# One non-local block and one attention block over four images: phi folded into theta, side work through one PSUM bank, one order of steps for all tiles

## The chip, the cores and the metric

The kernel runs on one core of one Trainium2 chip. The metric is the device time of one execution in microseconds (us), the median of several runs. The core has a matrix engine (TensorE; PE for its matmuls, PEld for its weight loads), VectorE (DVE), ScalarE (ACT), GpSimd (POOL) and SyncE (SP, which here only issues DMAs). Each engine works through its own list of instructions in order and waits on semaphores that the others raise.

## The reference

`x` is four images of 128 channels by 1024 pixels, float32. Two layers follow each other.

```python
# layer 0, per image, 64 inner channels, N = 1024
g_x     = conv1x1(x, g_w, g_b)^T          # N x 64
theta_x = conv1x1(x, theta_w, theta_b)^T  # N x 64
phi_x   = conv1x1(x, phi_w, phi_b)        # 64 x N
y   = (theta_x @ phi_x / N) @ g_x
z   = x + conv1x1(y^T, out_w, out_b)

# layer 1, per image, 128 channels
theta = conv1x1(z, theta_w, theta_b)
phi   = conv1x1(z, phi_w, phi_b)
scores = einsum('ncp,ncq->npq', theta, phi) / sqrt(128)
attn   = softmax(scores, axis=-1)
f      = einsum('npq,ncq->ncp', attn, z)
out    = z + conv1x1(f, conv1_w, conv1_b)
```

Layer 0 has no softmax, so it is an affine map of x once the 64 x 64 product phi_x g_x is known. Both kernels use that: Z = A x + d, with A and d made from that product for each image.

## The kernel before

**Layer 0 of an image.** `phi_g` (L208) multiplies the pixels with the joined phi and g weights; VectorE adds the bias into `pgT` (L660). `inner_product` (L219) forms the 64 x 64 product M; ScalarE copies it. `out_times_inner` (L230) and `fold` (L237 to L239) turn it into A (transposed) and d. `fold_x` forms A x; ScalarE writes `Z` (L535).

**Precision by splitting.** A float32 operand of a large matmul is split into a high part in the type fp32r and a low rest (`X_hi`, `X_lo`, and so on), and the product is made in three passes of fp32r (`three_passes`, L254). ScalarE or GpSimd writes the high part, VectorE or GpSimd the low part.

**Layer 1.** `theta` and `phi` make T and Phi from Z, each by three passes and each split again. The value matrix V (`values`, L262) is conv1_w applied to Z, so that the last convolution needs no work of its own. An image has eight tiles of 128 query pixels. For each tile t:

- PE `scores(t)`: six matmuls of 512 columns into a slot of `ring` (two banks to a slot);
- DVE `row_max` (L695) over 1024 columns, then ACT `exps` (L567), which writes `P` and the row sums, then DVE `norm` (L701, L703: reciprocal, then P times it);
- PE `turn` (L304): eight transposes of 128 x 128 into `turned`, in two halves of four;
- ACT `high_turned` (L576) and DVE `low_turned` (L710), one for each half, make `PT_hi` and `PT_lo`;
- PE `attend` (L334): after four tiles, a group, 24 matmuls of 512 columns in four pieces of six into `numer`; ScalarE copies `numer` to `attended`, GpSimd adds `Zres` (Z plus the bias) and SyncE stores.

**Order.** The lists of the engines are written out by hand. The side work for image b+1 (phi_g, M, R, A, A x, theta, phi) and V of image b stand between the tiles of image b. The middle images run in a hardware loop. PSUM is a `ring` of three slots of two banks (the third slot is split into `numer` and `small`) and `turned`. The side work takes ring slots 0 and 1 in turn with the scores, by the table `S_SLOT`. In a steady step the lists are:

- ACT: `high_turned(t-2, 0)`, `exps(t)`, `high_turned(t-2, 1)`;
- DVE: `row_max(t+1)`, `low_turned(t-1, 0)`, `norm(t)`, `low_turned(t-1, 1)`.

So a row maximum may be taken while the two engines are still at the transposes of an older tile, and the exponentials of a tile stand between the two high halves. PE stands up to two tiles of scores ahead (`scores(0)` to `scores(3)` of image 0 are issued before the first transpose). The last image's last group is finished by `attend_last` on 384 columns (L317) and a last tile in plain float32 (L495).

## Time and profile before

| | |
|---|---|
| median of 3 runs | 178.74 us (178.66 to 178.77) |
| span of the profiled execution | 176.7 us |
| PE busy | 170.2 us, 96% of the span |
| DVE busy | 131.4 us, 74% |
| ACT busy | 103.1 us, 58% |
| POOL busy | 35.8 us, 20% |
| chain that ended last | PE 83%, DVE 5%, ACT 5%, DMA 4% |

The profile is one execution. Its span runs from the first to the last instruction; the device time is about 2.0 us longer (178.74 less 176.7). Busy time of PE overstates its work, since a matmul's record also covers the pipeline behind it: what a matmul takes of the engine is read better from the distance between starts, which the chain of waits gives.

### The profile page before, as it was taken

The page shows a single profiled execution, that of the slowest core. Times are in us where ns is not written, and L with a number is a line of the kernel's source. Part 1 is how long each engine was busy: PE and PEld are TensorE (multiplying, and loading weights), DVE is VectorE, ACT ScalarE, POOL GpSimd, SP SyncE. Part 2 cuts the span into 40 slices and gives each one's busy share as a digit, 9 for nine tenths or more (in the row PEclk, how much of TensorE's full clock was granted, in tenths as well). Part 3 has the DMA queues.
Part 4 walks back from the last instruction along what each step waited for, and adds up shares of the span by engine and source line. Part 5 has one row for each costly group of instructions (what it writes and reads, how often), then busy time and mean ns, then how long its engine had stood idle before and what let it go on. Part 6 is the DMA issues. An engine that isn't in the chain of part 4 may idle for free.

```text
span 176.7 us, 2720 instructions
## 1 busy us (share of the span) xinstructions
PE 170.2 (96%) x974; PEld 138.9 (79%) x974; DVE 131.4 (74%) x189; ACT 103.1 (58%) x176; POOL 35.8 (20%) x32
## 2 busy tenths in 40 slices
PE   7899998999999999999999999999999999998994
PEld 7784585788889887888889787988888888876794
DVE  0315889886987776896988676796989689899811
ACT  3024477858683365958684274958686557656410
POOL 1105600003102200543202200443302202340000
PEclk9999999999999999999999999999999999999999
DMA  4600000003001000013001000010000100100011
GB/s 137 190 0 0 4 0 0 0 4 118 1 2 59 2 4 0 0 59 91 32 0 57 3 0 0 0 59 0 0 0 18 41 4 0 59 2 0 0 63 59
DMA packets 2537, 4.71 MB, mean 27 GB/s; under 512 B 288, under 2 KB 992, under 8 KB 2528
## 3 DMA queue, kind: packets, MB, share of 16 engines
q1 hardware_dynamic: 2096, 4.26, 7.1%
q10 hardware_dynamic: 432, 0.33, 0.8%
q8 instruction: 6, 0.10, 0.2%
q14 instruction: 3, 0.02, 0.1%
HBM read 2.49 MB, written 2.10 MB: 26 GB/s over the span
## 4 chain that ended last, share of the span: by engine, by line
PE 83%; DVE 5%; ACT 5%; DMA 4%; SPq 1%; issue 1%; ACTq 0%; DVEq 0%
PE ring L254 29%; PE ring L334 21%; PE turned L304 14%; PE ring L262 4%; DMA X<-x_dram 4%; ACT P L567 3%; PE ring L244 3%; PE ring L317 3%; PE ring L208 2%; DVE negmax L695 2%; DVE PT_lo L710 2%; ACT PT_hi L576 2%; PE ring L219 2%; PE turned L208 1%; PE ring L495 1%; PE ring L288 1%
## 5 line engine op out<-in xcount | busy, mean ns | idle before, releaser
L576 ACT ACTIVATE PT_hi<-turned 128x512 fp32r<-128x512 f32 x62 | 35.9, 595 | 26.5 <-PE turned L304 26.5
L695 DVE TENSOR_REDUCE negmax<-ring 128x1 f32<-128x1024 f32 x32 | 39.1, 1222 | 15.3 <-PE ring L254 15.1
L567 ACT ACTIVATE P<-ring,negmax 128x1024 f32<-128x1024 f32 x32 | 35.8, 1118 | 19.0 <-DVE negmax L695 19.0
L710 DVE TENSOR_TENSOR PT_lo<-turned,PT_hi 128x512 fp32r<-128x512 f32 x62 | 42.1, 684 | 5.2 <-ACT PT_hi L576 4.7
L304 PE MATMUL turned<-identity,P 128*128 128x128 f32 x256 | 36.1, 274 | 2.1 <-DVE P L703 1.6
L304 PEld LDWEIGHTS turned<-identity,P 128*128 128x128 f32 x256 | 30.4, 141 | 9.0 <-DVE P L703 1.6
L703 DVE TENSOR_SCALAR P<-P,rden 128x1024 f32<-128x1024 f32 x32 | 27.0, 845 | 1.1
L334 PE MATMUL ring<-PT_hi,V_hi 128*128 128x512 f32 x56 | 23.5, 420 | 0.1
L334 PE MATMUL ring<-PT_lo,V_hi 128*128 128x512 f32 x56 | 22.2, 396 | 0.0
L334 PE MATMUL ring<-PT_hi,V_lo 128*128 128x512 f32 x56 | 22.1, 395 | 0.0
L254 PE MATMUL ring<-Phi_hi,T_hi 128*128 128x512 f32 x62 | 21.3, 424 | 0.0
L254 PE MATMUL ring<-Phi_hi,T_lo 128*128 128x512 f32 x62 | 19.4, 394 | 0.0
L254 PE MATMUL ring<-Phi_lo,T_hi 128*128 128x512 f32 x62 | 19.3, 392 | 0.0
L835 POOL TENSOR_TENSOR result<-attended,Zres 128x512 f32<-128x512 f32 x6 | 8.6, 1432 | 37.4 <-ACT attended L583 37.4
L254 PEld LDWEIGHTS ring<-Phi_lo,T_hi 128*128 128x128 f32 x62 | 11.6, 188 | 2.7
L254 PEld LDWEIGHTS ring<-Phi_hi,T_lo 128*128 128x128 f32 x62 | 11.6, 188 | 2.7
L811 POOL TENSOR_TENSOR Z_lo<-Z,Z_hi 128x1024 fp32r<-128x1024 f32 x3 | 7.2, 2397 | 27.7 <-ACT Z_hi L541 27.7
L334 PEld LDWEIGHTS ring<-PT_hi,V_hi 128*128 128x128 f32 x56 | 10.5, 188 | 2.8 <-issue 0.6
L806 POOL TENSOR_TENSOR X_lo<-X,X_hi 128x1024 fp32r<-128x1024 f32 x3 | 7.1, 2367 | 26.9 <-ACT X_hi L527 26.9
L334 PEld LDWEIGHTS ring<-PT_hi,V_lo 128*128 128x128 f32 x56 | 10.5, 188 | 2.5
L254 PEld LDWEIGHTS ring<-Phi_hi,T_hi 128*128 128x128 f32 x62 | 10.1, 189 | 2.2 <-DVE T_lo L675 0.3
L334 PEld LDWEIGHTS ring<-PT_lo,V_hi 128*128 128x128 f32 x56 | 10.6, 189 | 1.6
(101 smaller groups left out, 200.3 us busy)
## 6 DMA issues: line engine op xcount, KB each, us to landing
out_dram<-result SPq DMA_DIRECT2D x7, 256.0 KB, 2.0
X<-x_dram SPq DMA_DIRECT2D x3, 512.0 KB, 3.3
X_first<-x_dram SPq DMA_DIRECT2D x2, 256.0 KB, 4.1
w<-weights_dram ACTq DMA_DIRECT2D x1, 194.0 KB, 5.8
out_dram<-result SPq DMA_DIRECT2D x1, 192.0 KB, 1.9
wi<-inner_dram SPq DMA_DIRECT2D x1, 64.2 KB, 5.9
pg_w<-pg_weights_dram ACTq DMA_DIRECT2D x1, 64.0 KB, 3.2
pg_b<-pg_bias_dram ACTq DMA_DIRECT2D x1, 64.0 KB, 5.5
```

Of the source, the lines that this page charges most:

```text
L254: mm = nc.tensor.matmul(ring[:, slot, columns(h)], left, right[:, columns(h)], start=(n == 0), stop=(n == 2))
L262: mm = nc.tensor.matmul(ring[:, slot, j * C:(j + 1) * C], Z[:, j * TILE:(j + 1) * TILE], w[:, W_C:W_C + C], start=True, stop=True)
L304: mm = nc.tensor.transpose(turned[:, j * TILE:(j + 1) * TILE], P[:, t % P_BUFFERS, j * TILE:(j + 1) * TILE], identity[:, :])
L334: mm = nc.tensor.matmul(numer[:, :], left[:, chunk], right[:, g, j, :], start=(j == 0 and n == 0), stop=(j == TILES - 1 and n == 2))
L567: nc.scalar.activation(P[:, t % P_BUFFERS, :], ring[:, slots[t], :], ACT.Exp, bias=negmax[:, t:t + 1], accum_out=den[:, t:t + 1]).then_inc ...
L576: nc.scalar.activation(PT_hi[:, g, half_chunks(h), k * TILE:(k + 1) * TILE], turned[:, columns(h)].rearrange("p (j r) -> p j r", j=CHUNKS_ ...
L695: nc.vector.tensor_reduce(negmax[:, t:t + 1], ring[:, slots[t], :], AX.X, ALU.max, negate=True).then_inc(max_ready, 1)
L703: nc.vector.tensor_scalar(P[:, t % P_BUFFERS, :], P[:, t % P_BUFFERS, :], rden[:, t:t + 1], None, ALU.mult).then_inc(probs_normed, 1)
L710: nc.vector.tensor_tensor(PT_lo[:, g, half_chunks(h), rows], turned[:, columns(h)].rearrange("p (j r) -> p j r", j=CHUNKS_PER_HALF), PT_hi ...
L806: nc.gpsimd.tensor_tensor(X_lo[:, :], X[:, :], X_hi[:, :].bitcast(F32), ALU.subtract).then_inc(x_lo, 1)
L811: nc.gpsimd.tensor_tensor(Z_lo[:, :], Z[:, :], Z_hi[:, :].bitcast(F32), ALU.subtract).then_inc(z_lo, 1)
L835: nc.gpsimd.tensor_tensor(result[:, g, :], attended[:, g, :], Zres[:, columns(g)], ALU.add).then_inc(result_ready, 1)
```

## The change

The kernel is written anew around the same arithmetic of A, Z, V and attention.

1. **Phi goes into theta.** The scores of a query p against all q are z_p^T (theta_w^T phi_w) z_q plus a term that depends on q alone plus terms constant in q. The kernel makes U = theta_w^T phi_w (scaled) once, at the start, with two transposes and a few small matmuls, and from then on `t = U^T Z + u` takes the place of T, and Z itself the place of Phi. The `phi` passes and `high_phi`/`low_phi` are gone. The term `rho` in p comes as an extra column of the V matmul (130 columns a chunk, one of them zero, instead of 128); a new VectorE instruction per tile combines it with the row maximum into `shift`, the bias of the exponential. (`shift` subtracts and adds `rho` again, and so carries the rounding of the maximum.)
2. **One bank for side work.** A bank `aux` of 512 columns takes all side work of the next image, in twelve jobs in a fixed order; each waits until the one before it is out of the bank (`aux_free`). The ring has two slots, for scores alone, used in turn. V of image b+1 is now made during image b, in three parts.
3. **One step for all tiles.** All 32 tiles run the same lists, unrolled. GpSimd now writes both parts of X and Z (`split_x`, `split_z`); `Zres` is gone, and the last bias is added when ScalarE copies `numer`.
4. **The first image** makes A x and t by three passes too (before: plain float32), and needs V for its first tile.

The core of the diff (the new three loops with what they call; "..." where lines are left out):

```diff
+JOBS = ("pg0", "pg1", "MT", "R", "A", "Z0", "Z1", "t0", "V0", "V1", "V2", "t1")
-        ring = ctx.enter_context(nc.psum_tensor("ring", [C, 3, PIX], F32))
-        S_SLOT = [1, 0, 1, 1, 0, 0, 0, 1]
+        ring = ctx.enter_context(nc.psum_tensor("ring", [C, 2, PIX], F32))
+        aux = ctx.enter_context(nc.psum_tensor("aux", [C, BANK], F32))
...
         def _(pe):
+            def job_pg(b, half):
+                pe.wait_ge(aux_free, aux_before(b, f"pg{half}"))
...
+            def scores(n):
...
+                if n >= 2:
+                    pe.wait_ge(probs_ready, n - 1)
+                for half in range(HALVES):
+                    if n == 0:
+                        pe.wait_ge(first_z_lo, half + 1)
+                    mm = scores_half(n, half)
+                mm.then_inc(scores_ready, 1)
+            def turn(n, half):
+                if half == 0:
+                    pe.wait_ge(probs_normed, n + 1)
+                if n >= 1:
+                    pe.wait_ge(turned_lo, (n - 1) * HALVES + half + 1)
...
+            job_t(0, 1)
+            pe.wait_ge(first_z_ready, 2)
+            scores(1)
+            for part in (1, 2):
+                pe.wait_ge(first_v_lo, part)
+                value_chunks(0, numer, part).then_inc(first_v, 1)
...
+            for n in range(ALL - 1):
+                b, t = divmod(n, TILES)
+                turn(n, 0)
+                if b + 1 < IMAGES:
+                    job_one(b + 1, t)
+                if n + 2 < ALL:
+                    scores(n + 2)
+                turn(n, 1)
+                if b + 1 < IMAGES:
+                    job_two(b + 1, t)
+                if n >= GT:
+                    attend(n // GT - 1, n % GT)
+            attend(ALL_GROUPS - 2, PIECES - 1)
...
         def _(act):
+            def exps(n):
+                t = n % TILES
+                if n >= P_BUFFERS:
+                    act.wait_ge(turned_ready, (n - P_BUFFERS + 1) * HALVES)
+                act.wait_ge(shift_ready, n + 1)
+                nc.scalar.activation(P[:, n % P_BUFFERS, :], ring[:, n % 2, :], ACT.Exp, bias=shift[:, t:t + 1],
+                                     accum_out=den[:, t:t + 1]).then_inc(probs_ready, 1)
...
+            high_t(0, 1)
+            exps(0)
+            exps(1)
+            first_v_high(1)
+            first_v_high(2)
...
+            for n in range(ALL - 1):
+                b, t = divmod(n, TILES)
+                high_turned(n, 0)
+                if b + 1 < IMAGES:
+                    job_one(b + 1, t)
+                high_turned(n, 1)
+                if b + 1 < IMAGES:
+                    job_two(b + 1, t)
+                if n + 2 < ALL:
+                    exps(n + 2)
+                if n >= GT and n % GT == GT - 1:
+                    copy_numer(n // GT - 1)
...
         def _(dve):
+            def row_max(n):
+                b, t = divmod(n, TILES)
+                dve.wait_ge(scores_ready, n + 1)
+                nc.vector.tensor_reduce(negmax[:, t:t + 1], ring[:, n % 2, :], AX.X, ALU.max,
+                                        negate=True).then_inc(max_ready, 1)
...
+                dve.wait_ge(max_ready, n + 1)
+                nc.vector.tensor_scalar(shift[:, t:t + 1], negmax[:, t:t + 1], rho[:, b % 2, t:t + 1],
+                                        rho[:, b % 2, t:t + 1], ALU.subtract, ALU.add).then_inc(shift_ready, 1)
...
+            first_z_low(0)
+            first_t_low(0)
+            first_z_low(1)
+            first_v_low(0)
+            first_t_low(1)
+            row_max(0)
+            low_t(0, 1)
+            row_max(1)
+            norm(0)
+            first_v_low(1)
+            first_v_low(2)
...
+            for n in range(ALL - 1):
+                b, t = divmod(n, TILES)
+                low_turned(n, 0)
+                if b + 1 < IMAGES:
+                    job_one(b + 1, t)
+                norm(n + 1)
+                if n + 2 < ALL:
+                    row_max(n + 2)
+                low_turned(n, 1)
+                if b + 1 < IMAGES:
+                    job_two(b + 1, t)
```

`job_one` and `job_two` are small functions that pick the side work of a step by its tile t, on each engine:

| t | PE one / two | ACT one / two | DVE one / two |
|---|---|---|---|
| 0 | pg0 / pg1 | none | pgT copy half 0 / half 1 |
| 1 | M / R | M copy / R copy | none |
| 2 | A / Z half 0 | high A / Z half 0 | d and low A / none |
| 3 | Z half 1 / t half 0 | Z half 1 / high t half 0 | none / low t half 0 |
| 4 | V part 0 / part 1 | high V 0 / high V 1 | low V 0 / low V 1 |
| 5 | V part 2 / t half 1 | high V 2 / high t half 1 | low V 2 / low t half 1 |

`attend`, `norm`, `high_turned` and `low_turned` do what they did before; `copy_numer` has become the instruction that also adds the bias.

## Rows read from the trace of the kernel before

**Rows 1.** The page: busy time per engine, and TensorE's granted clock in 40 slices.

```profile
PE 170.2 (96%) x974; PEld 138.9 (79%) x974; DVE 131.4 (74%) x189; ACT 103.1 (58%) x176; POOL 35.8 (20%) x32
...
PEclk9999999999999999999999999999999999999999
```

**Rows 2.** Chain that ended last, image 1 as current: start us, us, engine tile line.

```profile
53.27 1.78 PE ring L208 x16
55.05 0.87 PE turned L304 x8
55.92 1.38 PE ring L254 x6
57.30 1.41 PE ring L334 x6
...
65.15 1.08 PE ring L219 x16
66.23 1.59 PE ring L254 x6
...
70.09 0.41 PE ring L230 x2
...
72.97 1.79 PE ring L262 x16
...
75.90 1.58 PE ring L254 x6
...
93.54 1.78 PE ring L208 x16
```

**Rows 3.** Timeline, tile work of image 0: start us, us, engine, line, operation.

```profile
25.51 0.60 ACT L576 ACTIVATE PT_hi<-turned 128x512 fp32r<-128x512 f32 x1 [0.72 <-PE turned L304]
...
26.14 0.69 DVE L710 TENSOR_TENSOR PT_lo<-turned,PT_hi 128x512 fp32r<-128x512 f32 x1 [0.60 <-ACT PT_hi L576]
26.75 0.15 DVE L701 RECIPROCAL rden<-den 128x1 f32<-128x1 f32 x1
26.94 0.75 DVE L703 TENSOR_SCALAR P<-P,rden 128x1024 f32<-128x1024 f32 x1
...
28.33 1.21 DVE L695 TENSOR_REDUCE negmax<-ring 128x1 f32<-128x1024 f32 x1
...
29.58 1.12 ACT L567 ACTIVATE P<-ring,negmax 128x1024 f32<-128x1024 f32 x1 [0.53 <-DVE negmax L695]
...
30.69 0.59 ACT L576 ACTIVATE PT_hi<-turned 128x512 fp32r<-128x512 f32 x1
```

**Rows 4.** Chain that ended last, one turn through ACT and DVE in image 3.

```profile
158.92 1.21 ACT P L567 x2
...
162.56 1.21 ACT P L567 x2
```

**Rows 5.** The page: the group of the normalisation; count, busy us, mean ns of one.

```profile
L703 DVE TENSOR_SCALAR P<-P,rden 128x1024 f32<-128x1024 f32 x32 | 27.0, 845 | 1.1
```

**Rows 6.** Timeline, image 3: a GpSimd pass and the normalisation that runs beside it.

```profile
154.13 2.40 POOL L853 TENSOR_TENSOR V_last<-V_hi,V_lo 128x1024 f32<-128x1024 f32 x1 [0.75 <-DVE V_lo L689]
...
155.89 1.19 DVE L703 TENSOR_SCALAR P<-P,rden 128x1024 f32<-128x1024 f32 x1
```

**Rows 7.** Timeline, start: d of image 0, the first halves of T, the first transposes.

```profile
12.77 0.26 ACT L520 ACTIVATE d<-ring,w 128x1 f32<-128x1 f32 x1 [1.51 <-PE ring L239]
...
16.51 0.69 ACT L545 ACTIVATE T_hi<-ring,w 128x512 fp32r<-128x512 f32 x1 [2.18 <-PE ring L244]
...
17.23 0.75 DVE L675 SCALAR_TENSOR_TENSOR T_lo<-ring,w,T_hi 128x512 fp32r<-128x512 f32 x1 [0.62 <-ACT T_hi L545]
...
24.88 1.03 PE L304 MATMUL turned<-identity,P 128*128 128x128 f32 x8
```

**Rows 8.** Chain that ended last, its end: the last group and the last tile.

```profile
167.11 1.33 PE ring L317 x6
...
174.29 0.02 issue
```

More of the change, by code:

```diff
@@ L189, in _ @@
[L189 to L196 removed]
+            for half in range(HALVES):
+                sp.dma_start(X[:, 0, columns(half)], x[0, :, columns(half)]).then_inc(first_loaded[half], 16)
@@ new lines, in store @@
+            def store(b, g):
+                sp.wait_ge(result_ready, b * GROUPS + g + 1)
+                sp.dma_start(out[b, :, columns(g)], result[:, g, :]).then_inc(stored[g], 16)
+            load(2)
+            for b in range(IMAGES):
+                if b + 3 < IMAGES:
+                    load(b + 3)
+                store(b, 0)
+                if b < IMAGES - 1:
+                    store(b, 1)
+            b, g = IMAGES - 1, GROUPS - 1
+            for part, cols in enumerate((slice(0, LAST_COLS), slice(LAST_COLS, BANK))):
+                sp.wait_ge(last_ready, part + 1)
+                sp.dma_start(out[b, :, BANK + cols.start:BANK + cols.stop],
@@ new lines, in job_t, with value_chunks @@
+            def job_t(b, half):
+                pe.wait_ge(aux_free, aux_before(b, f"t{half}"))
+                if b:
+                    pe.wait_ge(z_lo, (b - 1) * HALVES + half + 1)
+                queries(b, aux[:, :], columns(half)).then_inc(aux_ready, 1)
+            def value_chunks(b, bank, part):
+                first, last = V_PARTS[part]
+                for j in range(first, last):
+                    at = (j - first) * V_COLS
+                    mm = nc.tensor.matmul(bank[:, at:at + V_COLS], Z[:, b % Z_BUFFERS, j * TILE:(j + 1) * TILE],
+                                          VW[:, :], start=True, stop=True)
+                return mm
@@ L306, in turn @@
                 mm.then_inc(turned_ready, 1)
-            def turn_tile(b, t, first=False):
-                for h in range(HALVES):
-                    turn(b, t, h, first)
-            def attend_last(j):
-                rows = slice(0, LAST_COLS)
-                chunk = slice(j * C, (j + 1) * C)
-                for n, (left, right) in enumerate(((V_hi, PT_hi), (V_hi, PT_lo), (V_lo, PT_hi))):
-                    mm = nc.tensor.matmul(last_rows, left[:, chunk], right[:, GROUPS - 1, j, rows],
-                                          start=(j == 0 and n == 0), stop=(j == TILES - 1 and n == 2))
-                return mm
```

1017 lines of the change are left out of this document (466 added, 551 removed).

## Prediction, made blind

> **What bounds the kernel now.** I read the page first. PE is busy for 96% of the span, and its granted clock stands at the full level in every slice [rows 1]. Busy time alone says little, so the chain of waits comes next: in the middle images it is one unbroken row of PE pieces, each starting where the last ended, from 53.27 to 93.54, which is one image, 40.27 us [rows 2]. Nothing but PE's work sets the time there. The distances give each piece's price: eight transposes 0.87, six score matmuls 1.38, six attention matmuls 1.41; phi_g 1.78, M 1.08, R 0.41, V 1.79, and A with d from 74.76 (where V ends) to 75.90, so 1.14 [rows 2]. Score matmuls right behind M or A take 1.6, some 0.2 more. In the first and the last image the chain leaves PE: it turns through ACT and DVE, and one such turn is 162.56 - 158.92 = 3.64 us a tile [rows 4], about what PE needs for a tile (0.87 + 1.38 + 1.41 = 3.66). So before the change the hand-made order holds two limits at almost the same height, and whatever lengthens the turn through ACT and DVE by a microsecond makes that turn the limit.
>
> **PE's own sum.** Gone are three times six matmuls of 512 columns for phi, 3 x 1.4 = 4.2 us, and image 0's float32 pass for it. Added: 2 columns in 130 for V, under 0.03 an image, and at the start two transposes and the small matmuls of U, near 1.3 us, which stand where R and A would wait anyway. Side work for one image is then 1.78 + 1.08 + 0.41 + 1.14 + 1.4 (A x) + 1.4 (t) + 1.8 (V) = 9.0 us. With eight tiles, 8 x 3.66 = 29.3, an image asks 38.3 us of PE, some 39 with the 0.2 behind each change of type, against 40.3 now. If PE stayed the bound, the kernel would win 1 to 2 us an image.
>
> **The turn through ACT and DVE.** Now the lists of the changed kernel. Step n on DVE is low half of turn n, norm(n+1), row_max(n+2), shift, second low half. On ACT it is high half of turn n, second high half, exps(n+2). Both are in order, which closes a ring: high(n,0) lets low(n,0) go; behind it in DVE's list stand norm(n+1) and row_max(n+2); shift(n+2) releases exps(n+2); and behind that in ACT's list stands high(n+1,0). No buffer opens this ring, since it lies in the order of the lists. The timeline gives each link as a distance between starts [rows 3]: high to low 26.14 - 25.51 = 0.63; low to reciprocal 0.61; reciprocal to multiplication 0.19; the multiplication 0.75, less the 0.08 by which a successor on the same engine may start early (0.69 against 0.61), 0.67; row maximum to exponential 29.58 - 28.33 = 1.25; exponential to the next high half 30.69 - 29.58 = 1.11. Together 4.46. The shift is new. Its nearest row is the reciprocal, as small (128x1), 0.15 and 0.19 to its successor; I take 0.19. It can't be below nothing, since the exponential waits for it; above I allow twice the reciprocal's distance, 0.38. Over 30 steps these ends are 6 us less and 6 us more. The ring is thus 4.65 us. The old turn of 3.64 held neither the norm nor the shift (0.86 + 0.19), and that is the difference: 3.64 + 1.05 = 4.69.
>
> The multiplication averages 0.845 over the kernel [rows 5] against 0.75 alone, and took 1.19 at 155.89, while GpSimd ran a pass from 154.13 to 156.53 [rows 6]. GpSimd now has more to do (both parts of X and Z), and the change puts the multiplication into the ring. I take 0.03 to 0.1 a step for it, ring 4.7. The Trainium skill, page "GPSIMD Engine Reference", says of the memory interfaces that they are shared with VectorE, with contention for its instructions in a two-port mode or with two SBUF inputs; by that rule every multiplication that meets one of GpSimd's passes would be slow, and none of the low halves (which read one operand from PSUM). The trace agrees on the multiplication. By the rule applied in full to GpSimd's longer day, 0.15 a step would be nearer than 0.05, 3 us in all.
>
> A step without side work is therefore 4.7 us and no longer 3.66: PE is idle for one microsecond in each.
>
> **What side work adds to the ring.** On DVE the first job of a step stands between low(n,0) and norm(n+1), so inside it. A pgT copy of 512 columns is as large as a low half, 0.61; low A with d, by the line through 0.15 (1 column) and 0.69 (512), 0.3; V parts 0 and 2, with the rho instruction, 0.6 and 0.45. That is 2.0 us an image. The copy of `numer` on ACT stands between exps and the next high half every fourth step: 0.5. The moves to GpSimd (high X, high Z) free ACT, which is not what the ring waits for. POOL's list has a store wait and 2 to 3 us passes, but it runs three jobs ahead of their use.
>
> **What the one bank adds.** PE may lag behind the ring by at most 4.65 - 2.3 - 0.7 = 1.7 us (norm(n+1) is done 2.3 after high(n,0), and a transpose half is readable 0.63 to 0.7 after it starts). Waits for `aux_free` eat that. I worked the lists through for one middle image, times from its first transpose, high(0,0) at 2.9:
>
> - t=0: pg0 is in the bank by 1.6, but DVE comes to its copy behind low(0,0) and frees it at 4.85. PE has stood at pg1 since 3.16 and everything behind it, attention and the next transposes, moves: they start at 7.15. The ring asks for 8.15 (2.9 + 4.65 + 0.6).
> - t=1: pg1 is freed behind row_max and the low half, at 8.3; M runs to 9.4, scores(3) behind it to 10.97, so row_max(3) starts at 11.07 in place of 10.3. R follows, PE turns the next tile at 13.4, high(2,0) at 14.1.
> - t=2 to 5: 19.8, 25.3 (with a `numer` copy), 30.5, 35.7; A's low part and V's low parts lie in the ring, and V2 waits 0.9 for V1. Then 40.4 and, with the second `numer` copy, 45.5.
>
> So a middle image takes 45.5 - 2.9 = 42.6 us, of which 8 x 4.7 + 2.0 + 1.0 = 40.6 are the ring and 2.0 the bank. Before: 40.3.
>
> **Start.** d of image 0 was ready at 12.77 [rows 7]; the chain to it is the same but for U, and the high and low parts of A are there at about 13.2. From there: first half of A x 0.95 (0.7 and the pipeline), Z high 0.69, Z low 0.75 [both rows 7], 15.6; t for tile 0, its two parts behind ACT's copy of Z, 16.9; second half of Z low 17.6; scores(0) readable 18.7. DVE then has in its list V's first part 19.2, t low 20.4, row_max 21.6, t low half 1 22.4, row_max(1) 23.7, norm 24.6. PE issues scores(1) by 21.8 and then stands at V part 2, which needs part 1's low half, which ACT begins only behind exps(1), at 24.9: 25.4, 26.0, V part 2 26.5, the first transposes 26.5 and high(0,0) at 27.2. Before, the first transposes were at 24.88 [rows 7], with two more tiles of scores behind them. The stop of PE here is hidden by nothing.
>
> **End.** From high(30,0): low, norm, second low, 2.9; then attend_last, the last turn and the last tile as now, 174.29 - 167.11 = 7.18 [rows 8]; then 176.7 - 174.29 = 2.4. Sum 12.4.
>
> **Sum.** Start 27.2; image 0 (side work but no attention in its first half, `numer` once) 40.8; images 1 and 2 2 x 42.6 = 85.2; tiles 24 to 29 6 x 4.7 + 0.5 = 28.7; end 12.4. Span 194.3, against 176.7 now. The device time is 2.0 above the span (178.74 - 176.7), so 196.3 us. The largest single loss is the last image: it has no side work left to hide in, and its eight steps go from 3.66 to 4.7.
>
> **Rivals.**
> PE stays the bound (the other side). Place: the steps of all images; it decides if high(n+1,0) does not in fact wait for exps(n+2), or if PE's queue of work fills the ring's idle time. Then start 26.5, 31 steps of tile work and three images of side work 135, type changes 3, end 7.2 + 2.4: span about 174, 176 us. The unbroken PE chain now speaks for it; the order of ACT's list against it. 3%.
> The ring without the bank: PE's waits are absorbed by its slack, steps at 4.65. Start 26.5, 30 x 4.65 = 139.5, `numer` 3, DVE's jobs 6, end 12.4: 187.4, 189.5 us. For it: 1.7 us of slack. Against: two jobs in one step need the bank freed twice by engines that come to it late. 17%.
> The bank costs more: each of the 18 steps with jobs is 0.4 longer than worked out, since the wait for the bank delays the scores and so the row maximum, as at t=1 above, or GpSimd's passes delay Z low and every multiplication. 194.3 + 7, 203 us. 15%.
> The clock falls: with PE idle a microsecond a step and 4 us at the start, the granted clock goes to 1.2 GHz, a tile costs PE 7.3 and the span grows by 31 x (7.3 - 4.7) = 80. In the trace the clock stays full through the idle of the first image [rows 1]. 2%. Beside this stands the Trainium skill, page "TensorE: Matmul & The Clock Gate", section "HAM oscillation", by which idle between bursts of matmuls throttles the engine again; gaps here are short and many.
>
> **How the numbers follow.** Forecast as summed 63%, within 191 and 200. The range takes in the light rival at 189 and most of the heavy one: 189 to 203. A difference under 0.2% can't be told from none. Faster only by the first rival, 3%; within 0.2% 1%; slower 96%.
>
> **What would show it.** Right: in tiles 24 to 29 high halves of new tiles start 4.6 to 4.8 us apart; the chain there runs ACT, DVE, DVE, DVE, ACT and hardly touches PE; the row maximum there waits for DVE's own list and not for PE; PE waits at `turned` for the norm; in steps with t=0 PE waits for pgT's copy; first high half at 27. Wrong: PE still unbroken in the middle images; a middle image under 41 or over 45; a clock below full.

## The result, and the profile after

The changed kernel takes 207.91 us (median of 4 runs, 205.63 to 208.72) against 178.75 for the kernel before: a ratio of 1.159 (95% interval 1.153 to 1.165; ratios here leave out executions more than 1.5% above the fastest of their kernel, in this case the one of 208.72). The forecast was 196.3 with a range of 189 to 203. The direction is right; the size is 4.9 us beyond the upper end. The profiled execution spans 206.2 us, where the sum said 194.3: 11.9 us are to be explained.

The page of the changed kernel (busy line; granted clock in 40 slices; the chain's shares by engine; two groups with count, busy us, mean ns | idle before and what ended most of it):

```profile
PE 174.5 (85%) x969; PEld 139.6 (68%) x969; DVE 139.4 (68%) x253; ACT 99.4 (48%) x183; POOL 35.4 (17%) x34
...
PEclk9999959999699987999999969999999999999999
...
DVE 37%; PE 36%; ACT 18%; issue 4%; DMA 2%; DVEq 0%; ACTq 0%; SPq 0%
...
L510 ACT ACTIVATE P<-ring,shift 128x1024 f32<-128x1024 f32 x32 | 35.7, 1116 | 48.6 <-DVE shift L669 48.5
...
L677 DVE TENSOR_SCALAR P<-P,rden 128x1024 f32<-128x1024 f32 x32 | 27.5, 861 | 1.1
```

PE has gone from 96% of the span [rows 1] to 85%. ScalarE stands for 48.5 us at the new shift instruction. And the clock, full in every slice before [rows 1], is not full in five.

The chain of waits in a stretch without side work (start us, us, what), where before stood an unbroken row of PE pieces [rows 2]:

```profile
61.81 1.21 ACT P L510 x2
63.02 0.50 ACT PT_hi L518
...
63.54 0.69 DVE PT_lo L684
64.23 0.08 DVE rden L675
...
64.33 0.75 DVE P L677
65.09 1.14 DVE negmax L661
...
66.33 0.28 DVE shift L669
...
66.70 1.21 ACT P L510 x2
67.90 0.50 ACT PT_hi L518
```

From one high half to the next (63.02 to 67.90) are 4.88 us, and no PE piece is among them: this is the ring that was forecast. The timeline of the same place shows the link that was not sized right (start us, us, engine, line, operation):

```profile
69.89 1.22 DVE L661 TENSOR_REDUCE negmax<-ring 128x1 f32<-128x1024 f32 x1
71.21 0.27 DVE L669 TENSOR_SCALAR shift<-negmax,rho 128x1 f32<-128x1 f32 x1
...
71.58 1.12 ACT L510 ACTIVATE P<-ring,shift 128x1024 f32<-128x1024 f32 x1 [2.70 <-DVE shift L669]
```

From the row maximum to the exponential are 1.69 us, against 1.25 before [rows 3]: the shift costs 0.44 in the ring, 0.27 for itself and the rest because it starts only when the maximum is out of the pipeline, 1.32 behind the maximum's start.

Where the 11.9 us lie, by the start of each image's first high half:

| stretch | forecast | measured | difference |
|---|---|---|---|
| start to high(0,0) | 27.2 | 27.7 | 0.5 |
| image 0 | 40.8 | 45.5 | 4.7 |
| images 1 and 2 | 42.6 each | 44.2, 44.3 | 3.3 |
| tiles 24 to 29 | 28.7 | 32.1 | 3.4 |
| end | 12.4 | 12.4 | 0 |

Two places stand out. In image 3 one multiplication takes 2.91 us beside a pass of GpSimd (timeline):

```profile
163.16 2.91 DVE L677 TENSOR_SCALAR P<-P,rden 128x1024 f32<-128x1024 f32 x1
...
163.17 2.35 POOL L829 TENSOR_TENSOR V_last<-V_hi,V_lo 128x1024 f32<-128x1024 f32 x1
```

It ends 0.55 behind GpSimd's pass (166.07 against 165.52), which is nearly its whole own length of 0.75. Before, the one that took 1.19 ended 0.55 behind the pass as well (157.08 against 156.53) [rows 6]. So it isn't slowed: it stands until the pass is over. That step takes 7.06 in place of 4.88. A pass that only casts does the same on a smaller scale:

```profile
91.80 0.61 POOL L805 CAST Z_hi<-Z 128x512 fp32r<-128x512 f32 x1 [0.53 <-ACT Z L485]
91.91 1.05 DVE L677 TENSOR_SCALAR P<-P,rden 128x1024 f32<-128x1024 f32 x1
```

Again the multiplication ends 0.55 behind the pass (92.96 against 92.41).

And PE stands at the second half of phi_g at the head of images 1 and 2, and then runs at half clock (timeline of PE; behind it the table of windows: us, busy by engine, granted clock, DMA share and GB/s):

```profile
72.80 0.60 PE L316 MATMUL turned<-identity,P 128*128 128x128 f32 x4
75.22 1.40 PE L226 MATMUL aux<-pg_w,X 128*128 128x128 f32 x8 [1.82 <-DVE pgT L625]
76.28 0.78 PE L336 MATMUL numer<-PT_hi,V_hi 128*128 128x512 f32 x1
76.85 0.63 PE L336 MATMUL numer<-PT_lo,V_hi 128*128 128x512 f32 x1
77.28 0.63 PE L336 MATMUL numer<-PT_hi,V_lo 128*128 128x512 f32 x1
```

```profile
26.00:36.00 10.00, 8.87 (x55) 7.93 (x55) 6.19 (x12) 3.34 (x7) 0.00 (x0) 0.72 0.03 5
52.00:56.00 4.00, 4.00 (x18) 3.46 (x16) 3.53 (x7) 0.97 (x3) 0.00 (x0) 0.57 0.00 0
61.00:71.00 10.00, 9.29 (x53) 7.35 (x52) 7.93 (x14) 4.71 (x9) 0.00 (x0) 1.00 0.00 0
73.00:83.00 10.00, 8.18 (x50) 6.54 (x48) 6.93 (x12) 3.42 (x8) 4.95 (x3) 0.83 0.07 26
```

The attention matmuls at 77 start 0.43 apart and not 0.23, so the clock is at the lower of its two levels, 1.2 and not 2.4 GHz. There are four such stretches inside the kernel, one of 6.8 us at the start and three of 3.4, at 52.1, 76.0 and 120.4: 17.1 us at half. The four executions don't share one clock: the one of 208.05 us, which is profiled here, had a mean clock of 0.957, the one of 205.63 had 0.975. The ordinary steps at 61 to 71, in which PE lacks more than a microsecond each (4.88 less 3.66) in pieces under 0.9 us, keep the full clock.

### The profile page after: what moved, and what is told of

It is laid out like the page before. It is cut to its first block, busy times and chain, and to the rows that moved or that the text cites. A ratio compares the mean times of both kernels' runs of the same rounds, so it can differ in the third digit from the quotient of the medians.

```text
span 206.2 us, 2628 instructions
## 1 busy us (share of the span) xinstructions
PE 174.5 (85%) x969; PEld 139.6 (68%) x969; DVE 139.4 (68%) x253; ACT 99.4 (48%) x183; POOL 35.4 (17%) x34
## 4 chain that ended last, share of the span: by engine, by line
DVE 37%; PE 36%; ACT 18%; issue 4%; DMA 2%; DVEq 0%; ACTq 0%; SPq 0%
DVE negmax L661 13%; ACT P L510 9%; PE numer L336 9%; DVE P L677 8%; DVE PT_lo L684 8%; ACT PT_hi L518 5%; PE turned L316 5%; PE ring L220 3%; DVE shift L669 3%; PE ring L221 3%; PE ring L222 3%; DMA X<-x_dram 2%; PE aux L343 2%; PE aux L226 2%; PE aux L232 2%
## 5 line engine op out<-in xcount | busy, mean ns | idle before, releaser
L684 DVE TENSOR_TENSOR PT_lo<-turned,PT_hi 128x512 fp32r<-128x512 f32 x62 | 42.6, 687 | 35.5 <-ACT PT_hi L518 35.5
L510 ACT ACTIVATE P<-ring,shift 128x1024 f32<-128x1024 f32 x32 | 35.7, 1116 | 48.6 <-DVE shift L669 48.5
L316 PE MATMUL turned<-identity,P 128*128 128x128 f32 x256 | 40.8, 284 | 9.7 <-DVE P L677 7.8
L220 PE MATMUL ring<-Z_hi,t_hi 128*128 128x512 f32 x64 | 28.4, 444 | 0.7 <-DVE t_lo L721 0.7
L336 PE MATMUL numer<-PT_hi,V_hi 128*128 128x512 f32 x56 | 25.0, 447 | 1.3 <-issue 0.7
L222 PE MATMUL ring<-Z_lo,t_hi 128*128 128x512 f32 x64 | 25.9, 404 | 0.0
L221 PE MATMUL ring<-Z_hi,t_lo 128*128 128x512 f32 x64 | 25.8, 403 | 0.0
L336 PE MATMUL numer<-PT_lo,V_hi 128*128 128x512 f32 x56 | 23.0, 411 | 0.0
L336 PE MATMUL numer<-PT_hi,V_lo 128*128 128x512 f32 x56 | 23.0, 411 | 0.0
L220 PEld LDWEIGHTS ring<-Z_hi,t_hi 128*128 128x128 f32 x64 | 12.4, 193 | 3.1 <-issue 1.1
L222 PEld LDWEIGHTS ring<-Z_lo,t_hi 128*128 128x128 f32 x64 | 12.4, 194 | 2.9
L221 PEld LDWEIGHTS ring<-Z_hi,t_lo 128*128 128x128 f32 x64 | 12.5, 196 | 1.6
```

Of the source, the lines that this page charges most:

```text
L220: nc.tensor.matmul(to, left_hi, right_hi[:, cols], start=first, stop=False)
L221: nc.tensor.matmul(to, left_lo, right_hi[:, cols], start=False, stop=False)
L222: return nc.tensor.matmul(to, left_hi, right_lo[:, cols], start=False, stop=last)
L316: mm = nc.tensor.transpose(turned[:, j * TILE:(j + 1) * TILE], P[:, n % P_BUFFERS, j * TILE:(j + 1) * TILE], identity[:, :])
L336: mm = nc.tensor.matmul(numer[:, :], left[:, b % 2, chunk], right[:, g, j, :], start=(j == 0 and n == 0), stop=(j == TILES - 1 and n == 2))
L510: nc.scalar.activation(P[:, n % P_BUFFERS, :], ring[:, n % 2, :], ACT.Exp, bias=shift[:, t:t + 1], accum_out=den[:, t:t + 1]).then_inc(pro ...
```

## The experiments

All ratios are to the kernel before. A "pure" step is one without side work and without a `numer` copy. Edits are to the changed kernel unless said otherwise.

**1. No side work.** All tiles use image 0's t, Z and V.

```diff
-                if b + 1 < IMAGES:
+                if False:
                     job_one(b + 1, t)
```

> The changed kernel without the side work for images 1 to 3 (no pg, M, R, A, Z, t, V for them; all 32 tiles use image 0's t, Z and V), so only the tile steps are left. Ring theory (high half, low half, norm, row maximum, shift, exponential, next high half, each behind the other by the order of two lists): a step stays at the 4.88 us of tiles 25 to 29 of the changed kernel, although PE needs only 3.66 for it; from high(0,0) to high(30,0) 30 x 4.88 + 6 x 0.57 for the numer copies = 149.8, with 2 more for the V_last pass, span 27.7 + 152 + 12.4 = 192, 194 us. PE theory: steps of 3.66, span 155. The difference to the changed kernel, about 14 us, is then all that side work, bank and lowered clock together cost. If the clock matters on its own, it falls here too, since PE idles more, and steps in the low stretches take 7 instead of 4.9.

193.93 us, 1.083 (1.078 to 1.087); pure steps 4.81, images 39.6. With nothing but the ring, the kernel is still 15 us slower than before, which alone rules out "PE stays the bound". Side work, its bank and what they do to the clock are the other 14. The clock itself is no fuller here (mean 0.955, five stretches of 3.4 us). Two of them, at 35.8 and 46.0, follow PE waits of 2.06 and 2.11 in steps that have no attention yet, and there they cost little: the two steps at 35.8 take 4.82 and 4.88, the one at 46.0 takes 5.29, where 4.81 is usual.

**2. Open the ring at ScalarE.** The exponentials go ahead of the second high half, one step later, as the kernel before had them.

```diff
                 high_turned(n, 0)
+                if n >= 1:
+                    exps(n + 1)
...
-                if n + 2 < ALL:
-                    exps(n + 2)
```

> The changed kernel with the exponential moved on ACT from behind both high halves of step n to behind the first high half of step n+1, where the kernel before has it. Ring theory: the ring opens; what is left is exponential, norm, row maximum, shift, exponential, 1.2 + 0.86 + 1.69 = 3.8 us. Steps 24 to 29 go from 32.1 us to 25 (with the V_last stop), images 0 to 2 by 2 to 3 each, down to what PE and the bank allow (41 to 42 an image): 190 to 194 us. Bank theory: under 3 us in all, since images 1 and 2 wait for the bank. Clock theory: PE idles less, so fewer low stretches.

189.36 us, 1.057 (1.052 to 1.062). Pure steps fall from 4.88 to 3.80, images to 39.0, 41.0 and 41.0. 18.5 us come back by moving one line in one engine's list, with every instruction kept: most of the loss is this order. In the chain, between the transposes of two tiles of image 3 (3.81 us), PE stands alone again:

```profile
159.60 0.44 PE turned L316 x4
160.04 0.23 PE ring L220
...
161.43 0.57 PE turned L316 x4
162.00 1.40 PE numer L336 x6
163.41 0.44 PE turned L316 x4
```

**3. No shift.** The exponential takes the row maximum itself as its bias.

```diff
-                act.wait_ge(shift_ready, n + 1)
-                nc.scalar.activation(P[...], ring[...], ACT.Exp, bias=shift[:, t:t + 1],
+                act.wait_ge(max_ready, n + 1)
+                nc.scalar.activation(P[...], ring[...], ACT.Exp, bias=negmax[:, t:t + 1],
...
-                nc.vector.tensor_scalar(shift[:, t:t + 1], negmax[:, t:t + 1], rho[...],
-                                        rho[...], ALU.subtract, ALU.add).then_inc(shift_ready, 1)
```

> The changed kernel without the shift instruction; the exponential takes the negated maximum as its bias. Ring theory: shift's link (row maximum to exponential is 1.69 us with it, 1.25 without) goes from every step: 4.88 to 4.44, tiles 25 to 29 by 2.2 us, and most of the other steps, 8 to 12 us in all: 196 to 200 us. If images 1 and 2 are bound by PE and the bank, only the 14 steps without side work gain, 6 us: 202.

197.73 us (193.2 to 198.74; the executions differ in where the clock falls, so no ratio is given). The pure step is 4.50, against 4.88: the ring without the shift was forecast at 4.46, and the shift is worth 0.38 a step. The timeline, one round from low half to low half:

```profile
61.30 0.69 DVE L676 TENSOR_TENSOR PT_lo<-turned,PT_hi 128x512 fp32r<-128x512 f32 x1 [0.56 <-ACT PT_hi L518]
61.91 0.15 DVE L667 RECIPROCAL rden<-den 128x1 f32<-128x1 f32 x1
62.09 0.75 DVE L669 TENSOR_SCALAR P<-P,rden 128x1024 f32<-128x1024 f32 x1
62.76 1.22 DVE L661 TENSOR_REDUCE negmax<-ring 128x1 f32<-128x1024 f32 x1
63.90 0.68 DVE L676 TENSOR_TENSOR PT_lo<-turned,PT_hi 128x512 fp32r<-128x512 f32 x1
65.80 0.69 DVE L676 TENSOR_TENSOR PT_lo<-turned,PT_hi 128x512 fp32r<-128x512 f32 x1 [1.22 <-ACT PT_hi L518]
```

**4. The ring in the kernel before.** Its own arithmetic, slots and side work, but both vector engines' lists in the changed order.

```diff
                 for t in range(TILES - 1):
-                    row_max(b, t + 1, slots)
                     if t >= 1:
                         low_turned(b, t - 1, 0)
                     norm(b, t)
+                    row_max(b, t + 1, slots)
...
                     high_turned(b, t - 2, 0, has_prev)
+                    high_turned(b, t - 2, 1)
                     exps(b, t, has_prev, slots)
```

> The kernel before with nothing but the order of two lists changed to that of the changed kernel: on ACT the exponential behind both high halves, on DVE the norm ahead of the row maximum. Phi, slots and side work as before. Ring theory: the ring high, low, norm, row maximum, exponential (no shift here) takes 4.44 to 4.50 us; the last image's tiles go from 3.66 to 4.5, 6 us for eight; in images 0 to 2 PE needs 40 and the ring 8 x 4.5 = 36 plus about 4 for DVE's own side work inside it, so 0.5 to 1.5 more each: 185 to 189 us, and PE's unbroken chain is broken in the last image. If the loss came from the single bank or the first image, the order alone costs nothing: 179.

222.14 us, 1.244 (1.242 to 1.246). The pure step in the last image is 4.51, as in experiment 3, so the ring belongs to the order and not to the new arithmetic. But the whole was missed by over 30 us: images of 47.5, 51.2 and 49.7. With side work in the ring's own two slots, the late exponentials also hold those slots, and single steps take up to 8.7: PE waits up to 3.73 us for an exponential there. The clock also falls six times (mean 0.953); how much of the 30 us it makes isn't separated. With this order, the separate bank does better than the shared slots.

**5. Row maximum ahead of the norm.**

```diff
-                norm(n + 1)
                 if n + 2 < ALL:
                     row_max(n + 2)
+                norm(n + 1)
```

> The changed kernel with the row maximum and shift ahead of the norm on DVE. Ring theory: the ring to the exponential loses the norm (0.86) and falls to 4.02, but the transposes of the next tile now come behind row maximum and norm: 0.62 + 0.61 + 1.32 + 0.19 + 0.19 + 0.79 + 0.66 = 4.4 us a step becomes the ring. 0.48 less in the steps without side work, nearly as much in the others: 195 to 200 us. Against: if PE or the bank bound images 1 and 2, only 14 x 0.48 = 7 us at the most from image 3 and tiles 6 and 7.

207.8 us, 1.153 (1.144 to 1.162): nothing gained. Pure steps fall only to 4.60, and steps with side work grow (6.23 and 6.49 for t=0 and 1 of image 1). The chain of waits says why:

```profile
66.31 0.66 PE turned L316 x4
66.97 0.23 PE ring L220
...
68.12 0.25 PE ring L222
...
68.39 1.24 DVE negmax L661
...
69.72 0.27 DVE shift L669
70.00 0.08 DVE rden L675
...
70.10 0.76 DVE P L677
...
70.91 0.66 PE turned L316 x4
```

The norm now stands behind a row maximum that waits for PE's scores, and PE's next scores stand behind the transposes that wait for the norm. ScalarE is out of the ring, PE has come in, and that ring is 4.60.

**6. V_last late.** GpSimd makes it behind the last norm.

```diff
-                else:
-                    pool.wait_ge(aux_free, aux_after(i, "V2"))
-                    nc.gpsimd.tensor_tensor(V_last[:, :], ...).then_inc(v_joined, 1)
                 if i >= 1:
                     finish((i - 1) * GROUPS + 1)
+                if i + 1 == IMAGES:
+                    pool.wait_ge(probs_normed, ALL)
+                    nc.gpsimd.tensor_tensor(V_last[:, :], ...).then_inc(v_joined, 1)
```

> The changed kernel with GpSimd's V_last pass moved behind the last norm. In the changed kernel the multiplication that started at 163.16 beside this pass took 2.91 us and ended 0.55 behind it. If VectorE's multiplication can't run while GpSimd holds the memory interface, step 24 goes from 7.06 to 4.9 and the kernel gains 2.2: 205.7 us. If the 2.9 us had another cause, no change.

207.73 us, 1.163 (1.161 to 1.165). Step 24 falls from 7.06 to 4.90, so the stop of 2.2 us is shown. The time doesn't follow: the end takes 13.7 and not 12.4, and a new stretch at half clock lies there, at 191.6. That stretch need not come from the move. It follows a PE wait of 1.46 us, and behind the same wait one lies in experiment 8 too, where V_last stands in its old place and the end takes 13.8; in the changed kernel's trace the wait is there and the stretch is not.

**7. Idle matmuls before each turn.** PE is kept busy with 6 small matmuls ahead of each wait for the norm, and 60 at the start. They write into `turned`, so the wait for the last low half now stands ahead of them.

```diff
                 if half == 0:
+                    if n >= 1:
+                        fill(6)
                     pe.wait_ge(probs_normed, n + 1)
```

> The changed kernel with idle matmuls of 128 columns on PE (results overwritten): six ahead of each wait for the norm, sixty ahead of the wait for V part 2 at the start. Clock theory: the granted clock falls four times in the changed kernel (17.1 us at half), and its four runs give 129 us for 1.0 of mean clock, so 5.6 us for the 0.043 missing; with PE filled the clock stays full and the time is 202 to 203, unless the 0.35 us of filling per step delays the side work. Ring theory alone: no change beyond 1 us, since PE waits for the ring at either clock. If the drops come from the waits for the bank and not from those for the norm, they stay.

207.16 us, 1.156 (1.153 to 1.160); mean clock 0.974 in place of 0.957. Image 0 gets 1.2 shorter, image 1 stays at 44.3: t=0 falls to 5.70, but the filling delays later steps by 0.5 and less. Inconclusive on the clock's price, so experiment 13 puts the filling elsewhere.

**8. First copy of pgT ahead of the low half.**

```diff
+                if b + 1 < IMAGES and t == 0:
+                    job_one(b + 1, t)
                 low_turned(n, 0)
-                if b + 1 < IMAGES:
+                if b + 1 < IMAGES and t > 0:
                     job_one(b + 1, t)
```

> The changed kernel with DVE's copy of pg half 0 ahead of the low half of the same step. Bank theory: the copy leaves the ring (0.61) and PE no longer stands at pg half 1 (from 73.2 to 75.2 in image 1), M comes earlier and with it scores and row maximum of t=1: step t=0 from 6.6 to 5.0, t=1 from 5.5 to 5.2, 2 us an image, 6 in all, and the low stretches of the clock at 76 and 120 go: 201 to 202 us. If the bank costs nothing beyond the copy in the ring: 2 us in all, 206.

212.04 us, 1.185 (1.182 to 1.189): slower, the opposite of what was expected. t=0 falls from 6.58 to 5.72, and t=1 rises from 5.51 to 7.18. PE's wait has moved to the next job, and the half clock with it (timeline of PE, where M takes 1.73 and not 1.15):

```profile
80.51 1.73 PE L232 MATMUL aux<-pgT 128*64 128x64 f32 x16 [2.05 <-DVE pgT L625]
```

Of the 4.4 us by which this profiled execution is longer, images 1 and 2 make 1.5. The other 2.9 are start and end (high(0,0) at 29.2, end 13.8), where its trace has stretches at half clock, at 12.6 and 196.9, that the changed kernel's has not.

**9. Attention ahead of the second job.**

```diff
+                if n >= GT:
+                    attend(n // GT - 1, n % GT)
                 if b + 1 < IMAGES:
                     job_two(b + 1, t)
-                if n >= GT:
-                    attend(n // GT - 1, n % GT)
```

> The changed kernel with PE's attention piece ahead of the second job of each step in place of behind it. Bank theory: PE's wait for the bank (2.0 us at pg half 1, up to 1 at V part 2 and t half 1) is covered by the 1.4 us of attention, the next transposes are no longer late: t=0 from 6.6 to 5.9, t=2, 4 and 5 by 0.1 to 0.3; 1 to 1.5 us for images 1 and 2, nothing for image 0's first half: 205. Ring theory alone: under 1 us, since the ring sets the step and PE has slack.

216.37 us, 1.208 (1.201 to 1.215). Missed again, and instructive: t=0 falls to 5.74, but t=1 is 7.80, t=2 5.63 and t=3 6.24. The attention piece is what PE has to do while the second job gets out of the bank; ahead of it, two jobs stand with too little between them, and PE waits 2.05 us at the same M as above. So "attention last" is the right order for the one bank.

**10. Ring open and no shift** (edits 2 and 3 together).

> The changed kernel with the exponential back between the high halves and without shift. Ring theory: what is left of the ring is 3.80 - 0.38 = 3.42 us, below PE's 3.66, so steps without side work go to 3.66 and PE's chain closes there; steps with side work, 5.1 to 6.1 with the exponential alone moved, lose up to 0.3 each: 2 + 3 to 5 us below the 189.4 of that kernel: 183 to 186. If ring and bank were additive in full, 0.38 x 30 = 11: 178.

185.21 us, 1.024 (1.019 to 1.030). Pure steps 3.66, which is PE's own price for a tile: the ring is gone. In the profiled execution (186.53 us) the start is long, high(0,0) at 29.0 (29.9 in experiment 2), with two stretches of 6.8 us at half clock. One execution kept the full clock throughout and took 182.35.

**11 and 12. A shorter start.** V part 2 of image 0 moves into step 1 on all three engines, so that PE no longer waits ahead of the first transposes until part 1 is out of its bank; this on top of edits 2 and 3 and together with edit 9; then the same with 16 and 24 idle matmuls in the start.

```diff
+            first_values(1)
...
                 if b + 1 < IMAGES:
                     job_two(b + 1, t)
+                if n == 1:
+                    first_values(2)
```

> The changed kernel with the exponential back between the high halves, without shift, with attention ahead of the second job, and with V parts 1 and 2 of image 0 taken out of the way of the first transposes (part 2 goes into step 1). Start: high(0,0) from 27.7 to 24.5 or 25; images 0.5 to 1 us less each than without the last two edits: 178 to 181, about the kernel before. Rival: the V parts come back as waits in steps 0 and 1, and the gain of the start is given back there.

> As mid_vlate, with idle matmuls in the two idle stretches of PE at the start (sixteen before t of tile 0, twenty-four before the first transposes). Clock theory: the low stretches behind the start (6.8 us at 24.8 in the changed kernel) go, 1.5 to 2 us less than without, and the runs scatter less. If PE had slack there, no change.

184.72 us, 1.034 (1.032 to 1.036), and 185.12, 1.037 (1.033 to 1.040). high(0,0) comes at 24.3, but each middle image takes 41.8 in place of 40.2: edit 9 loses 3.2 us of the 4.8 that the start of the profiled executions gained. At full clock it loses more than the start gives, since the four executions of experiment 11 were all at full clock and took 184.4 to 185.1, against the one of 182.35 above. In neither trace is there a stretch at half clock, so the idle matmuls had nothing to mend there.

**13. Filling exactly where PE stands.** 60 idle matmuls in the start, 30 ahead of the second pg job, into the free ring slot.

```diff
                 if t == 0:
+                    n = (b - 1) * TILES
+                    pe.wait_ge(probs_ready, n + 2)
+                    for _ in range(30):
+                        nc.tensor.matmul(ring[:, (n + 1) % 2, 0:C], idle[:, :], idle[:, :], start=True, stop=True)
                     job_pg(b, 1)
```

> The changed kernel with idle 128-column matmuls on PE in two places where it stands long: 60 of them behind the wait for V part 1 at the start, 30 (into the free ring slot) ahead of the second pg job of each image, where PE waits for VectorE's copy of pgT. No wait and no order is changed. Theory A (the lowered clock costs some 0.9 us for each of the stretches at 52, 76 and 120 us and 1 to 1.8 at the start): the granted clock stays full, step t=0 goes from 6.6 to 5.7, image 0 from 45.5 to 43.5, and the time from 207.9 to 203 to 204.5. Theory B (the ring would wait anyway, the clock only falls where PE has time): the clock stays full and nothing moves by more than 1 us, 207 to 208.5. If the clock still falls somewhere, only the stretches that are gone tell.

205.22 us, 1.144 (1.140 to 1.147). PE of this kernel at the head of image 1 (timeline):

```profile
72.14 1.84 PE L421 MATMUL ring<-idle 128*128 128x128 bf16 x30
74.13 1.16 PE L226 MATMUL aux<-pg_w,X 128*128 128x128 f32 x8 [0.15 <-DVE pgT L632]
75.04 0.48 PE L336 MATMUL numer<-PT_hi,V_hi 128*128 128x512 f32 x1
75.36 0.39 PE L336 MATMUL numer<-PT_lo,V_hi 128*128 128x512 f32 x1
```

PE waits until the same moment of the step, but the clock stays full behind it: t=0 takes 5.71 in place of 6.58, and images 1 and 2 take 43.5 and 43.6 in place of 44.2 and 44.3. Each stretch of 3.4 us at half there costs 0.7. Image 0 gains 1.0, the start 0.1. Filling thus gives back 2.5 us in the trace and 2.7 in the medians. That is not all that the clock costs: one stretch is left, at 49.7 in image 0, behind another wait of 2.11, and one lies at 12.2, ahead of the filling, where the trace of the changed kernel has none but those of experiments 2, 8, 9, 10 and 16 have one as well.

**14 to 16. What is left when ring and start are free.** Experiment 10 with V part 2 of image 0 and V_last late, attention last; then also without the `rho` column and its VectorE instructions; then that with V_last in its old place.

```diff
-                    mm = nc.tensor.matmul(bank[:, at:at + V_COLS], Z[...], VW[:, :], start=True, stop=True)
+                    mm = nc.tensor.matmul(bank[:, at:at + C], Z[...], VW[:, 0:C], start=True, stop=True)
...
-                nc.vector.tensor_scalar(rho[...], chunks_of(bank, part)[:, :, C:C + 1], r0, None, ALU.add)
```

> The kernel with the exponentials between the two high halves and without the shift instruction (mid_noshift), and besides V parts 1 and 2 of image 0 moved behind the first turns, and V_last made behind the last normalisation; the attention piece stays last in each step. If the attention piece behind the second job is what covers a job's way out of the bank, the images are again 38.3, 40.1 and 40.1 (not 41.8 as with attention ahead of the second job), the first high half comes at 24.3, step 24 goes from 5.2 to 3.8, and the end takes up to 1 us more: span 179.4, 181.4 us. If instead the early start itself costs the images their cover, they stay near 41.8 and the time near 183.5.

> open_vlate without the rho column: V is made of 128 columns a chunk, and the three rho instructions of VectorE for each image are gone (without shift nobody reads rho). Theory (VectorE's jobs stand in the ring at their full price): 3 x 0.19 an image less, 1.8 us in all, 179.6. If PE and the bank set these steps, VectorE's small instructions were hidden: no difference above 0.5 us from open_vlate. The kernel before is at 178.8; either result leaves it at least even.

> open_norho with V_last made where the changed kernel makes it (GpSimd's pass beside the normalisation of tile 25). If VectorE's multiplication is stopped while GpSimd's pass runs, step 24 is 5.2 again in place of 3.8 and the end is shorter by up to 1: 180 us. If with the ring open the stop is covered, it is no slower than open_norho, 179 to 179.6.

179.35 us, 1.006 (1.002 to 1.009); 178.56, 1.002 (0.998 to 1.005); 180.59, 1.012 (1.005 to 1.018). The images are 37.2, 40.1 and 40.2, then 37.1, 39.9 and 39.9: attention last covers the bank. Taking out the rho column is worth 0.6 us, not 1.8 (the executions at full clock have medians of 179.0 and 178.4, those at a mean clock of 0.981 of 180.9 and 180.3). With V_last in its old place step 24 is 5.16 and not 3.46, so the stop of 1.7 us stays even with the ring open, and V_last late costs nothing here: the end is 13.6 in both. (Its profiled start is 1.0 later, 25.2 against 24.2, with a stretch at half clock at 12.3.) The page of the second:

```profile
PE 163.0 (92%) x969; PEld 134.8 (76%) x969; DVE 127.5 (72%) x209; ACT 99.0 (56%) x183; POOL 35.3 (20%) x34
...
PEclk9999999999999999999999999999999999999999
```

The new arithmetic with one bank and one step for all tiles is therefore even with the kernel before. None of the sixteen beats it by more than the measurement can tell.

## Why the prediction was right and wrong

**The mechanism of the main loss was right.** The ring high, low, norm, row maximum, exponential, high is in the chain of waits, with ACT and DVE alone; its links without the shift were forecast at 4.46 and measured at 4.50 (experiments 3 and 4); opening it brought pure steps to 3.80, and to PE's 3.66 without the shift. The end was forecast at 12.4 and is 12.4; the stop of PE at V part 2 in the start is there, 3.65 us, and high(0,0) came 0.5 later than worked out. Step 24 and the larger shift apart, the last image paid as said. Two of the signs that the prediction named went against it: the high halves start 4.88 apart, where 4.6 to 4.8 was to show it right, and the clock is below full.

**The term that was mis-sized: the shift.** It was taken as a reciprocal, 0.19, with 0.38 as its upper end. In the changed kernel the link grew by 0.44, and taking the instruction out gave 0.38 a step. What failed is the choice of row. The reciprocal's 0.19 is the price of an operation whose operand had long been there; the shift needs the row maximum's result, so the part of the 1.22 us record that a successor may overlap is paid again, and its own record is 0.27 long. Over 30 steps the excess of 0.25 is 7.5 us. Less what the other links and the unused allowance for GpSimd gave back (0.07 a step), 5.4 us of the 11.9 remain as its share.

**GpSimd beside the multiplication** was averaged to 0.03 to 0.1 a step. It is one stop of 2.2 us in step 24, shown by experiment 6, and the row that tells it had been read: a multiplication that ends 0.55 behind GpSimd's pass [rows 6]. It should have been priced as the rest of the pass. Five more multiplications meet a cast of X or Z and take 0.96 to 1.12, together 1.3 us, which is 0.04 a step and within what was taken; the group's mean of 861 ns hardly moved from 845 [rows 5]. The Trainium skill (page "GPSIMD Engine Reference", section "Specifications") tells of contention on interfaces that GpSimd shares with VectorE. The trace agrees that the multiplication is held and that the low halves are not (0.69 beside a pass and alone); the evenly spread 0.15 a step that the prediction made of it is not how the cost comes here.

**The clock** was given 2% and 80 us, all or nothing, and nothing in the sum. The all didn't come: an idle microsecond in every step left the clock full. What came is partial: PE stands for some 2 us at one place in an image, and a stretch of 3.4 us at half follows (6.8 in the start). Experiment 13 gave back 2.4 to 2.7 us of it, with two stretches left. The executions of the changed kernel point higher: from 0.957 to 0.975 of mean clock the time falls by 2.4 us, and this slope, carried on to a full clock, gives 5.6 (an estimate, as worked out ahead of experiment 7). So the clock costs 2.4 us at least and 5.6 by this slope, and no run fixes it between them. Experiments 8 and 9 show the same wait and the same half clock moved to M.

**The bank** was forecast at 2.0 us a middle image. At full clock (experiment 13) the middle image is 43.5 where the forecast plus the larger shift gives 42.6 + 1.4 = 44.0, so it was half a microsecond too dear. Image 0 was the reverse. It was taken as 1.8 cheaper than a middle image, because it has no attention in its first half, and in experiment 13 it was 1.1 dearer (44.6 against 43.5), with one stretch at half clock left in it, at 49.7. Its fifth step takes 7.01 against 5.49: PE stands 2.11 at V part 0, with no attention piece ahead of it, and the clock falls. Experiment 9 shows what a missing piece does elsewhere; for image 0 itself this is argued and not tested. Some 2.3 us of image 0's 4.7 are left when the larger shift (1.4) and what filling gave back (1.0) are taken off, and the parts of clock and bank in them stay open.

**The sum after all:** start 0.5, shift 5.4, stop 2.2, clock 2.4, image 0 2.3, less 1.0 for the middle images: 11.8 of 11.9 us. Shift and stop, 7.6 us, rest on runs that took the one or the other away. The 2.3 of image 0 is a remainder and not a price that was measured, so that the sum closes is no evidence for it: if the clock costs more than the 2.4 put down here, the rest shrinks by as much. The step of the prediction that failed is therefore in three terms of its sum: the shift at 0.19 where 0.44 was measured, GpSimd's pass spread over all steps where it is one stop of 2.2 us, and the clock at nothing.

**PE's own sum** was 38.3 to 39 for an image. In experiment 15 a middle image takes 39.9, against 40.27 before [rows 2], so of the forecast gain of 1 to 2 us an image 0.4 is seen. But 39.9 isn't PE's sum alone: the chain there leaves PE and runs through VectorE and ScalarE for 6.4 us ahead of V part 2 (82.09 to 88.52) and for 9.3 us from the end of image 1 to M in image 2 (97.28 to 106.56). What folding phi would give with PE alone as the bound no run shows.

## What to carry over

Write the lists of all engines beside each other and follow each step's output through the order of the lists: a ring closed by order is as hard as one closed by data, no buffer opens it, and moving one line may be worth more (18.5 us here) than the arithmetic saved. Price an instruction that enters such a ring by a row in which it needs its predecessor's result, and price a wait of the matrix engine by what the engine still has in its list behind it. When one wait is taken away, ask which job has the next one: three of the moves tried here (5, 8 and 9) only passed it on.

## What the runs showed of the hardware

A VectorE multiplication by a pointer scalar, 128x1024 in float32 from SBUF to SBUF, stands still beside a GpSimd pass over SBUF tensors. In fourteen of the eighteen kernels here, the one before among them, the multiplication beside V_last took between 1.19 and 3.00 us, and in each it ended 0.55 us behind the pass, whenever it had begun. A cast from one SBUF tensor does the same: in all eighteen traces 76 multiplications began behind a GpSimd pass that had over 0.1 us to go, and each ended 0.5 to 0.6 us behind that pass. It works the other way too: in experiment 3 a cast that began 0.08 us behind a multiplication (129.08 against 129.00) took 1.15 us and not 0.61.

The granted clock fell in pieces of 3.4 us or twice that. In the changed kernel the four stretches began 0.8 to 1.5 us after a PE wait of 1.82 to 3.65 us ended or while it ran. But the length of one wait doesn't decide it: 2.57 us up to 166.12, beside V_last, was followed by no such stretch, while at the same wait in experiments 1, 3, 7 and 8 (2.29 to 2.65 us) one began, and in experiment 6 one began at 191.6 behind a wait of 1.46. Where the stretches lie differs from one execution of a kernel to the next. A stretch of 3.4 us cost from 0.1 us (at 35.8 in experiment 1) over 0.7 (the heads of images 1 and 2) and 1.0 (the start, experiment 16 against 15) to 1.3 (the end, 13.7 against 12.4 us), each time less than the 1.7 by which PE falls back in it; where PE had slack, the ring set the time anyway. Idle time in many pieces under 0.9 us left the clock full, and behind thirty small matmuls in the gap no stretch followed (experiment 13, images 1 and 2).
